# Decoder block with routed experts on one core: a scratch tensor laid out by sequence, rank counts in the shared work banks, and the order of the last routing steps

## The reference

```python
S, B, _ = x.shape                       # here S = 8 sequences, B = 512 positions
# y = LN(x + mha(x)), attention over the 8 sequences at one position
xf = y.reshape(S * B, D)                # D = 256
logits = xf @ Wg.T                      # 8 experts
idx = jnp.argmax(logits, axis=-1)
for e in range(8):
    m = (idx == e)[:, None]
    h = relu(xf @ W1[e] + b1[e])        # 256 -> 1024
    out = out + m * (h @ W2[e] + b2[e]) # 1024 -> 256
z = LN(y + out)                         # x + z is the result
```

## Time and profile before

| what | value |
|---|---|
| runs | 1168.07, 1165.09, 1165.38 us |
| profiled run | 1168.07 us, span 1166.1 us, granted PE clock 0.988 |
| PE busy | 1086.4 us (93%) |
| DVE busy | 730.0 us (63%) |
| POOL busy | 507.9 us (44%) |
| ACT busy | 472.2 us (40%) |
| q1, the DMA queue of SP | 38.0% of 16 engines |

### The profile page before, as it was taken

How to read it: one execution, slowest core, us unless ns; L and a number is a source line. 1 busy time by engine, 2 the same in 40 slices (tenths; PEclk the granted TensorE clock), 3 DMA queues, 4 the chain that set the end, 5 groups by cost and what they waited for, 6 DMA issues and landing times. The chain is left out here.

```text
span 1166.1 us, 29237 instructions
## 1 busy us (share of the span) xinstructions
PE 1086.4 (93%) x9964; PEld 739.9 (63%) x9965; DVE 730.0 (63%) x2074; ACT 472.2 (40%) x866; POOL 507.9 (44%) x757
## 2 busy tenths in 40 slices
PE   8999899999999999999989989999889999999995
PEld 3546455464464554644644556666659999999994
DVE  4655776757857767577545545777835566665553
ACT  5434545454544454445453234333213333333330
POOL 3324525235245262453342032554445555555654
PEclk9999999999999999999999999999989999999998
DMA  7273563735545637346385144544131111111110
GB/s 219 72 211 107 148 184 99 206 104 150 158 123 163 176 99 200 100 132 169 105 213 149 44 150 144 189 141 160 52 113 47 45 50 45 53 54 53 55 38 8
DMA packets 144373, 137.86 MB, mean 118 GB/s; under 512 B 31912, under 2 KB 137646, under 8 KB 144176
## 3 DMA queue, kind: packets, MB, share of 16 engines
q1 hardware_dynamic: 138192, 124.12, 38.0%
q0 software_dynamic: 5280, 12.66, 3.3%
q10 hardware_dynamic: 832, 0.16, 0.1%
HBM read 49.30 MB, written 50.83 MB: 86 GB/s over the span
## 5 line engine op out<-in xcount | busy, mean ns | idle before, releaser
L980 ACT ACTIVATE probs<-ps_ab 128x512 f32<-128x512 f32 (+2 forms) x352 | 175.0, 540 | 85.7 <-PE ps_ab L1301 36.3
L600 POOL TENSOR_SCALAR_AFFINE_SELECT probs<-probs 128x512 f32<-128x512 f32 x128 | 83.5, 652 | 258.3 <-ACT probs L980 254.0
L2912 PE MATMUL ps_ab<-e_yT,e_w_now 128*128 128x128 f32 x1248 | 147.5, 277 | 0.0
L2912 PEld LDWEIGHTS ps_ab<-e_yT,e_w_now 128*128 128x128 f32 x1248 | 144.2, 194 | 0.5 <-ACT e_yT L2883 0.4
L2923 PE MATMUL ps_c<-keep_w,e_hT 128*128 x624 | 141.0, 379 | 0.0
L2923 PEld LDWEIGHTS ps_c<-keep_w,e_hT 128*128 128x128 f32 x624 | 115.7, 190 | 14.1
L721 DVE CUSTOM_DVE_ANT_0 ps_ab<-ps_ab,mask_qk 128x256 f32<-128x256 f32 x224 | 89.3, 451 | 14.8 <-PE ps_ab L1271 14.6
L1844 ACT ACTIVATE e_w_now<-keep_w 128x1024 f32 x78 | 78.2, 1049 | 33.0 <-DVE keep_expert_table L2406 20.6
L715 DVE TENSOR_REDUCE top<-ps_ab 128x2 f32<-128x512 f32 (+1 forms) x112 | 74.2, 684 | 25.8 <-PE ps_ab L1271 24.2
L1271 PE MATMUL ps_ab<-k_rows,q_rows 96*128 96x256 bf16 (+1 forms) x512 | 84.5, 260 | 6.3 <-DVE top_prefix L707 2.9
L2847 DVE TENSOR_SCALAR e_hT<-ps_ab,keep_b 128x128 f32<-128x128 f32 x312 | 84.5, 343 | 9.0 <-PE ps_ab L2912 6.9
(11 more groups left out here) (250 smaller groups left out, 2094.8 us busy)
## 6 DMA issues: line engine op xcount, KB each, us to landing
sorted_rows<-filler SPq DMA_DIRECT2D x8, 4290.0 KB, 17.9
q_rows<-parts SPq DMA_DIRECT2D x96, 128.0 KB, 2.4
k_rows<-parts SPq DMA_DIRECT2D x96, 128.0 KB, 2.4
q_rows<-q_parts SPq DMA_DIRECT2D x96, 128.0 KB, 2.4
keep_w<-in_e_w SPq DMA_DIRECT2D x16, 512.0 KB
keep_w<-in_e_w SPq DMA_DIRECT2D x8, 1024.0 KB
e_row<-sorted_rows SPq DMA_DIRECT2D x39, 130.0 KB, 2.0
x_in<-in_x SPq DMA_DIRECT2D x8, 512.0 KB, 4.1
```

The source lines that it names most:

```text
L600: nc.gpsimd.affine_select(own, own, [[0, TILES], [1, P]], ALU.is_ge, keep_zero, base=0, channel_multiplier=-1).then_inc(probs_cut.sem, 1)
L980: nc.scalar.activation(probs[:, user % 2, lo:lo + width], ps_exp[:, f % 2, 0:width], ACT.Exp).then_inc(exp_done.sem, 1)
L2912: mm = nc.tensor.matmul(ps_h[s][:, f // 4, (f % 4) * P:(f % 4 + 1) * P], w1_now[:, s, k, f * P:(f + 1) * P], yT[:, s, k * P:(k + 1) * P], ...
```

## The change

Three things change, and they are independent of each other in the code.

First, `x2_rows` is laid out sequence first, [8, 512, 256]. A row's place in it is then its place in the output, so one number per row is kept in place of two: POOL's start has one copy in place of five small instructions, `number_rows` writes one column, and the expert stage uses the same number for gather and scatter. `load_x`, for groups 1 to 7, becomes eight DMAs of 64 KB (one per sequence, 16 partitions each) in place of one of 512 KB.

Second, the rank counts go through the two work banks, as the last fill of a pass. The waits that guarded the spare corner go.

Third, at the end of the mixing stage POOL sends group 6 before its pass 7, and two tiles of group 7 before its pass 8, in place of all of group 6 and one tile of group 7 there. DVE chooses for group 7 after the first two `mix` of group 8 and makes its slots after the statistics of group 8. PE makes all four outputs of group 8 before the ranks of group 7.

```diff
-                    sp.dma_start(x_in[:, :, :], t["x2"].rearrange("(g c i) s d -> g (i s) c d", g=NGROUPS, c=TILES)[m]
-                                 ).then_inc(x_loaded.sem, 16)
+                    for s in range(B):
+                        sp.dma_start(x_in[s:P:B, :, :],
+                                     t["x2_groups"][m, s].rearrange("(c i) d -> i c d", i=POS)).then_inc(x_loaded.sem, 16)
...
-ROUTE_FILLS = ["out0", "out1", "out2", "out3"]
+ROUTE_FILLS = ["out0", "out1", "out2", "out3", "ranks"]
+LAST_FILLS_MIX = ["out0", "out1", "out2", "out3", "ranks_held", "ranks"]
-MIX_FILLS = ["xT0", "xT1", "out0", "out1", "out2", "out3", "q0", "q1", "k0", "k1", "v0", "v1", "v2", "v3"]
+MIX_FILLS = ["xT0", "xT1", "out0", "out1", "out2", "out3", "q0", "q1", "k0", "k1", "v0", "v1", "v2", "v3", "ranks"]
+CLOSING_FILLS = ["out0", "out1", "out2", "out3"]
...
-                "v": (v_ready, TILES + k + 1), "out": (mixed_ready, k + 1),
+                "v": (v_ready, TILES + k + 1), "out": (mixed_ready, k + 1), "ranks": (next_row_ready, k + 1),
+                "ranks_held": (next_row_ready, 0),
...
-                    nc.gpsimd.tensor_copy(rows[:, (n - 1) % 2, :, D:D + 2], origin[:, :, :]).then_inc(token_written.sem, 1)
+                    nc.gpsimd.tensor_copy(rows[:, (n - 1) % 2, :, D], token[:, :]).then_inc(token_written.sem, 1)
...
                 for n in range(2, NGROUPS):
-                    if n < NGROUPS - 1:
-                        send_rows(n - 1)
+                    send_rows(n - 1)
                     iteration(n, ahead=n < NGROUPS - 1, more=n < NGROUPS - 2)
-                send_rows(NGROUPS - 2)
-                send_rows(NGROUPS - 1, (0,))
+                send_rows(NGROUPS - 1, (0, 1))
                 iteration(NGROUPS, ahead=False, more=False)
-                send_rows(NGROUPS - 1, (1, 2, 3))
+                send_rows(NGROUPS - 1, (2, 3))
                 send_rows(NGROUPS)
...
                     mix(n, 0)
                     mix(n, 1)
-                    slots(n - 1)
+                    choose(n - 1)
                     mix(n, 2)
                     mix(n, 3)
                     post_norm_statistics(n)
+                    slots(n - 1)
                     post_norm_scale(n)
...
-                    if n > 1:
-                        pe.wait_ge(next_row_ready.sem, next_row_ready.count(n - 1, 1))
...
                 def ranks(n):
 
-                    pe.wait_ge(oT_ready.sem, oT_ready.count(min(n, NGROUPS - 1), KD))
-                    if n > 1:
-                        pe.wait_ge(next_row_ready.sem, next_row_ready.count(n - 1, 1))
+                    ps = work_claim(pe, n, "ranks")
                     pe.wait_ge(chosen_ready.sem, chosen_ready.count(n, 1))
...
-                output(NGROUPS, (0, 1))
+                output(NGROUPS)
                 ranks(NGROUPS - 1)
-                output(NGROUPS, (2, 3))
...
-                        in_offset=bass.IndirectOffsetOnAxis(ap=token[:, u % UNROLL, 1:2], axis=0), bounds_check=B * S - 1,
+                        in_offset=bass.IndirectOffsetOnAxis(ap=token[:, u % UNROLL, :], axis=0), bounds_check=B * S - 1,
...
-    t["x2"] = nc.dram_tensor("x2_rows", [S, B, D], F32, kind="Internal").ap()
+    t["x2"] = nc.dram_tensor("x2_rows", [B, S, D], F32, kind="Internal").ap()
+    t["x2_groups"] = t["x2"].rearrange("s (g p) d -> g s p d", g=NGROUPS)
```

67 lines of the change are left out of this document (29 added, 38 removed).

## The result

The changed kernel takes 1183.37 us (median of 4 runs, 1179.50 to 1187.26), against 1165.78 us for the kernel before on the same chip (4 runs, 1165.09 to 1168.07). The ratio is 1.014, 95% interval 1.0099 to 1.0182. The forecast was 1170.7 us: slower was right, the size was not; 5.3 us were forecast and 12 to 18 us came.

The account below looks back on a forecast made before the run. The prediction took PE to bound the kernel, with the change acting in the 193.6 us mixing stage. Border waits 3.5, eight loads 1.2 and the end 0.6 us gave 1165.4 + 5.3 = 1170.7 us, range 1166 to 1176.5.

Parts of the forecast that it names:

- the sum 3.5 + 1.2 + 0.6 = 5.3 us: Mixing stage: new wait at the borders 3.5, eight loads 1.2, end of the stage 0.6 us, added to the median.
- What bounds the kernel: PE bounds attention and expert stages; the change lives in the mixing stage, three borders set by PE, three by or near load/DVE.
- the 0.8 us that this border was to absorb: At the 769 us border, taken as load-bound, PE's 1.44 us pause would cover 0.84 us of new wait.
- The wait of xT1: At five borders the fifth transpose waits for the add into m_next_row: 0.86 us each, 4.3 in all, 3.5 after absorption.
- The eight loads: Loads of x_in between passes: issue hidden behind the expert weights, 0.4 us at three borders, 1.2 us; bounds 0 to 5.3.
- The clock: Rival at the borders: added pauses lower PE's clock, three more falls of 1.8 us, 1176.1 us; chance 0.15.
- The end: End of mixing stage: rstd of group 8 starts 1.9 us later, one send fewer saves 1.3: net +0.6, bounds -1.3 to +2.9.
- Layout: Stores of x2 and gathers of the expert stage change only addresses, beside PE work: 0, at most 1 us either way.
- The load carries it: Rival: borders at 710, 729 and 769 us, set by the load, absorb the wait; +1.0 us, 1166.4; chance 0.22.

Follow-up runs that it names:

- after_again: The changed kernel unaltered, run again on a second chip against the kernel before: 1179.95 us against 1168.32, ratio 1.0105.
- load_first_old: The kernel before with the load of x_in issued ahead of the expert weights: 1166.72 us against 1167.07, ratio 0.9998 to the kernel before.
- load_first_new: The changed kernel with the eight loads of x_in issued ahead of the expert weights: 1171.10 us, ratio 1.0046 to the kernel before.
- old_layout: The changed kernel with the old layout, one load of 512 KB and two numbers to a row: 1170.13 us, ratio 1.0025 to the kernel before.
- layout_only: The kernel before with only the sequence-first layout, one number per row and eight loads per group: 1172.50 us, ratio 1.0024 to the kernel before.
- eight_only: The kernel before with only the load of x_in cut into eight DMAs of 64 KB, old layout: 1174.72 us, ratio 1.0071 to the kernel before.
- warm_fill: The changed kernel with eight unneeded matmuls filling PE's wait before xT1 from the second border on: 1175.17 us, ratio 1.0074 to the kernel before.
- end_only: The kernel before with only the new order at the end of the mixing stage: 1167.90 us, ratio 1.0000 to the kernel before.
- both_fixes: The changed kernel with the eight loads ahead of the weights and DVE's slots ahead of the shift: 1169.75 us, ratio 1.0016 to the kernel before.

## Why the prediction was wrong in size

The step that failed is the sum 3.5 + 1.2 + 0.6 = 5.3 us: it adds the wait of the ranks and the late loads as if each cost the same with and without the other. The runs show 1.0008, 1.0024 and 1.0000 for the parts alone, 3.7 us together, but 1.0075 for the first two in one kernel and 1.0105 and 1.0140 (12 and 18 us) for all three. The term that was mis-sized is the fall of the clock: the sum has it at nothing, the rival at 1.8 us a fall, and with the new wait behind it a fall costs 3.2 us. Take away the late load and the wait, and 1.0016 is left.

*What bounds the kernel: right in the stage, wrong at the borders.* The mixing stage carries the loss (14.9 of 15.4 us in the profile of after_again), and most of it is lost at the borders. But the 769 us border was taken as set by the load because PE pauses 1.44 us there. The same pause stands at 811 us, which was taken as set by PE, and in load_first_old, where the load is early. So no run shows the 0.8 us that this border was to absorb.

*The wait of xT1: right in place and nearly in size.* It came at all five borders. out0 is 0.71 us later (2.25 against 1.54), the first queries 0.62 us (5.87 against 5.25), where 0.86 was put: handing over took 0.05 us and not 0.15, and the small waits of out0 for ACT (0.25 us in the earlier trace rows) went. load_first_new against load_first_old, in which no border falls, has 29.91 - 27.22 = 2.7 us over the five borders; the forecast's term was 3.5. old_layout (ranks and end: 3 us, 0.5 to 5.4) agrees with 3.5 + 0.6.

*The eight loads: priced too low.* They were put at 1.2 us, at most 5.3, because the issue was thought to hide behind the weights and the last piece to land 2.6 us after its issue. As the change has them, with the new layout, they cost 2.8 us (0.6 to 5.1, layout_only), inside the bounds. Out of the old layout eight_only measured 0.71%, 8.3 us (5.4 to 11.3), above even the upper bound. Two errors: the landing of 2.6 us was read from pieces that ran with nothing ahead of them and behind the weights is 5.7 us (median), with issues of 5.1 to 7.1 us in place of 4.8 (DVE's waits for x_in are no measure of this: 21.6 us in all after, 25.7 before); and the price was taken as lateness alone, us for us, while two borders of the eight_only profile fall, against one before. The Trainium skill (DMA: Bandwidth & Descriptors, Bandwidth), which the forecast weighed and set aside, advises against such a cut; the runs side with its advice, though not with eight transfers one after another. That the rows themselves lie elsewhere is not at fault: layout_only, with the new rows, is at 1.0024 and eight_only, with the old ones, at 1.0071. The two ran on different chips, and why the old ones are the worse is open.

*The clock: named as a rival with 0.15, and priced at 1.8 us a fall.* The 1.8 came from the earlier trace rows, where PE was busy behind the transposes and the clock came back within the outputs. With the wait of xT1 behind the fall it doesn't: outputs of 5.4 to 5.6 us, 9.05 - 5.87 = 3.2 us a fall. That holds where the fall begins at the ranks; at 772 us in the profile after it begins within the wait, and the outputs take 4.83 us (7.32 - 5.87 = 1.5 us). The forecast had the wait as the thing that makes the clock fall; load_first_new shows a wait of 0.89 us without a fall, and warm_fill that the wait prolongs one. The terms were added, and they multiply: the loads have a part in how often the clock falls, the ranks in how long it stays down. The sum for after_again is 5 x 0.6 + 3 x 3.2 = 12.6 us over borders that lose nothing. Over those of the kernel before, which lose 1.8 us themselves, it is 10.7 us, and its six passes and the next are 14.4 us longer than before. The 3.7 us between lie outside the stretch from the ranks to the queries: 1.45 us of them are PE's wait for the choice ahead of the first of these borders, the rest I did not trace. What sets off a fall stays open. With the load behind the weights, 15 of the 60 borders in twelve profiles fall; with the load first, none of 20 in four. These four profiles are of executions at or below the median of their kernels, and executions of the same kernels took up to 1181.44 us, so none is not proven for them. The Trainium skill (TensorE: Matmul & The Clock Gate, HAM oscillation — how this bites in real kernels) describes a kernel in which bursts of about 2 us are parted by waits of 3 to 5 us for a DMA and the clock falls at every one. The pauses here are 0.8 to 2 us, and three of five borders fall at most.

*The end: right in the order, and inside its bounds.* From the ranks of group 6 to those of group 8 end_only takes 24.89 us against 23.09, and from there to the first load of the expert stage 10.04 against 11.58: +0.3, where +0.6 was forecast. Over all profiles this stretch has 36.1 us with the new order and 34.8 with the old one, +1.3, and what was not forecast, the expert stage gives 1.6 us back. By time the two can't be told from nothing (end_only 1.0000, 0.9973 to 1.0028). The upper bound of +2.9 leaves out the 1.3 us of the send that goes; with it, it would be +1.6. In the profile of the changed kernel the stretch has 3.2 us more. The heads there take 4.75 us for 128 matmuls in place of 1.67, of which 1.6 us are the four pauses; no other of the sixteen profiles has them. No run here tells where they come from.

*Layout: 0, as far as can be told.* both_fixes bounds all that is left, layout and end together, to 0.3%. The attention stage is 1.1 us longer on average with it, within the spread of the profiles.

*"The load carries it" (0.22) was the wrong way round.* A border set by the load was thought to absorb the wait. In after_again the borders behind a wait of DVE for the load are the ones that cost most.

## What to carry to other kernels

Before adding a short wait to an engine, look at what else is late at the same place. Here the wait alone cost 0.6 us and a fall of TensorE's clock alone 1.4 to 1.8; a fall with the wait behind it cost 3.8 (9.0 us in place of 5.25). A load cut in eight behind bulk in its queue cost 2.8 to 8.3 us here. In the changed kernel it paid to put the load that somebody waits for ahead of the bulk that nobody does (1.0046 in place of 1.0105, intervals that overlap); in the kernel before it made no difference (0.9998). Before reading a pause as a wait, look whether it stands at the same instruction in a kernel where nothing is late.

## What the runs showed of the hardware

A granted clock that had fallen came back early when PE stayed busy: in warm_fill the windows read 0.50 and then 0.94.

```profile
773.60:776.40 2.80, 2.80 (x20) 2.01 (x17) 2.70 (x11) 0.60 (x1) 0.00 (x0) 0.50 0.67 174
776.40:780.80 4.40, 4.40 (x23) 3.60 (x22) 2.20 (x8) 1.12 (x2) 2.89 (x3) 0.94 1.04 367
```

It was low there from about 773.6 to 776.8 us. With one idle us in the middle it stayed low for 7 us (from 814.8 to about 821.7 us in the profile after).

A pause as such does not tell whether the clock falls. 1.44 us given to no releaser stand before a border with a fall and, in the same profile at 811 us and in load_first_old at 769 us, before borders without one. These pauses stand inside the scores, at the third border in every profile and at the fifth in all but one (0.8 to 1.5 us), whatever the edit; what they are is open.

The time of an execution goes with its mean granted clock: of the eight executions of the changed kernel in the first comparison (the profiled ones among them) the quickest has 1175.36 us at 0.987 and the slowest 1187.26 us at 0.979. Where the clock is lost, two profiles of this kernel show: at 0.985 the mixing stage takes 202.52 us, at 0.981 (after_again) 209.41, with an expert stage of 299.8 and 300.5 us.

How PE enters a stage shows in its first us: filled up to the first load of sorted rows and past it, the expert stage has a granted clock of 1.00 in its first 5 us in all ten profiles with the new order; with the filling over before it, 0.59 to 0.90 in the six others, and the stage is 1.6 us longer on average.
